# A graph-network kernel: in the edge-embedding pass TensorE makes the second product of the last group before the first product of the new one

## What is computed

```
def _mlp(h, W1, b1, W2, b2, g, beta):
    h = silu(h @ W1 + b1)
    h = silu(h @ W2 + b2)
    mu = mean(h, axis=-1); var = mean(square(h - mu), axis=-1)
    return g * (h - mu) * rsqrt(var + 1e-5) + beta

edge_attr = _mlp(edge_attr, emb_W1, emb_b1, emb_W2, emb_b2, emb_g, emb_beta)
...
agg = segment_sum(edges_new, dst)
```

## Time and profile before

| what | value |
|---|---|
| median of 3 runs | 4343.94 us (4342.17 to 4346.43) |
| the profiled execution's own time | 4335.36 us |
| span of its trace | 4333.6 us |
| share of the span: PE, DVE, ACT, POOL | 73%, 59%, 31%, 49% |
| the embedding pass, from PE's first product to ACT's last instruction | 195.7 to 679.6 us |

### The profile page before, as it was taken

The page is one execution under the profiler, slowest core; times in us unless marked ns, Lnnn a source line. Parts: engine busy times, 40 slices in busy tenths (PEclk is TensorE's granted clock), DMA queues, the critical chain, the costliest instruction groups (busy, mean ns, idle before and its releaser), DMA issues. The chain is left out here.

```text
span 4333.6 us, 75781 instructions
## 1 busy us (share of the span) xinstructions
PE 3180.2 (73%) x18633; PEld 2208.0 (51%) x18633; DVE 2559.6 (59%) x9494; ACT 1355.3 (31%) x2970; POOL 2130.8 (49%) x2173
## 2 busy tenths in 40 slices
PE   2488884669999997499998589998555555655554
PEld 1366662226666664377777367776333333333332
DVE  7678885986555563688887667776632222422223
ACT  0077875950111100255555345555300000200000
POOL 0477771000000001377775277776357777177776
PEclk7588987999999998599999799999755555755555
DMA  2112222000000002366666254455121212422223
GB/s 59 41 55 69 75 67 103 2 7 24 17 16 17 17 15 67 107 169 181 179 181 141 65 150 129 130 132 109 26 64 53 53 53 53 136 53 53 53 53 52
DMA packets 248988, 327.58 MB, mean 76 GB/s; under 512 B 78191, under 2 KB 159678, under 8 KB 247806
## 3 DMA queue, kind: packets, MB, share of 16 engines
q1 hardware_dynamic: 180410, 206.68, 15.5%
q0 software_dynamic: 68256, 117.02, 12.5%
HBM read 230.66 MB, written 92.83 MB: 75 GB/s over the span
## 5 line engine op out<-in xcount | busy, mean ns | idle before, releaser
L2520 PE MATMUL gat_acc<-gat_rows,gat_hot 128*128 128x128 f32 x1664 | 574.6, 478 | 486.0 <-issue 245.4
L2520 PEld LDWEIGHTS gat_acc<-gat_rows,gat_hot 128*128 128x128 f32 x1664 | 400.3, 317 | 661.6 <-issue 660.9
L992 PE MATMUL hop_p_a<-hop_h,adj 128*128 128x384 bf16 x4375 | 712.9, 327 | 0.0
L992 PEld LDWEIGHTS hop_p_a<-hop_h,adj 128*128 (+1 forms) x4375 | 428.5, 98 | 284.1 <-issue 1.7
L1928 POOL DMA_INDIRECT lb_far<-far_rows,lb_idx x416 | 405.6, 975 | 195.8 <-issue 117.0
L2503 POOL DMA_INDIRECT gat_rows<-typed_rows,gat_idx x416 | 395.7, 951 | 214.0 <-DVE gat_idx L2528 87.6
L2503 POOL DMA_INDIRECT gat_rows<-hidden_rows,gat_idx x416 | 395.2, 950 | 196.8 <-PE gat_acc L2520 77.4
L1928 POOL DMA_INDIRECT la_far<-far_rows,la_idx x416 | 409.7, 985 | 154.4 <-issue 117.9
L1650 POOL DMA_INDIRECT by_src_records<-scatter_rec,scatter_rank x375 | 376.9, 1005 | 128.9 <-issue 102.4
L2536 DVE TENSOR_SCALAR gat_hot<-iota_row,gat_tabs 128x128 f32<-128x128 f32 x416 | 147.7, 364 | 370.5 <-PE gat_acc L2520 364.4
L2533 DVE TENSOR_SCALAR gat_hot<-iota_row,gat_tabs 128x128 f32<-128x128 f32 x416 | 124.6, 305 | 392.6 <-PE gat_acc L2520 382.5
(11 more groups left out here) (498 smaller groups left out, 6418.9 us busy)
## 6 DMA issues: line engine op xcount, KB each, us to landing
edge_features<-emb_out SPq DMA_DIRECT2D x104, 256.0 KB
la_feat<-edge_features SPq DMA_DIRECT2D x104, 256.0 KB
edge_features<-la_out SPq DMA_DIRECT2D x104, 256.0 KB
lb_feat<-edge_features SPq DMA_DIRECT2D x104, 256.0 KB
la_place<-dst_row SPq DMA_DIRECT2D x104, 128.0 KB
lb_place<-dst_row SPq DMA_DIRECT2D x104, 128.0 KB
typed_rows<-gat_typed_row SPq DMA_DIRECT2D x25, 512.0 KB
hop_side<-x0share_nodes SPq DMA_DIRECT2D x125, 64.0 KB, 1.8
```

The source lines that it names most:

```text
L992: ins = nc.tensor.matmul(p_a[(u.par + r) % 2][:, 0:3 * D], K.adj[:, s, bass.ds(u.t * P, P)], h3[r % 2][:, s, :, :].rearrange("p i d -> p ( ...
L2520: nc.tensor.matmul(acc[:, bass.ds(at[u % LOADS], D)], hot[u % HOTS][:, :], rows[u % RING][:, :], start=False, stop=True, skip_group_check= ...
```

## The change

In each turn of PE's loop, `second(g-1)` is issued before `first(g)`; it was the other way round. The waits inside the two functions go with them. Nothing else is altered.

```
             for g in range(max(GE + SUM_LAG, ALL + 1)):
+                if 1 <= g <= ALL:
+                    second(g - 1)
                 if g < ALL:
                     first(g)
-                if 1 <= g <= ALL:
-                    second(g - 1)
                 if 0 <= g - SUM_LAG < GE:
                     third(g - SUM_LAG)
```

## The result

The changed kernel takes **4360.75 us** (median of 7 runs, 4359.49 to 4361.83). The kernel before, run again beside it, takes 4342.17 us (7 runs, 4335.14 to 4352.06). The ratio is 1.0041, with a 95% interval of 1.003 to 1.0052: 18.6 us slower, where 17.0 were forecast. The profiled execution took 4361.62 us, its span is 4359.8 us (4333.6 before).

A forecast was written before the change was run, and what follows sets the result against it. No engine is full in the middle of the pass; DVE was taken as pace maker. Losses of 5.9 + 10.1 + 1 = 17.0 us, added to the median 4343.94, gave 4360.9, taken as 4361 us, range 4348 to 4376.

The forecast's parts named there:

- The mechanism: On ACT, rows(g-1) is queued behind hidden(g), whose input now comes last; at both ends no third fills PE's gap.
- the three terms: Losses at start, middle and end of the pass: 5.9 + 10.1 + 1 = 17.0 us.
- Start: First six turns: PE waits for hidden(g) with no third between, 3.95 us a turn instead of 2.97; 5.9 us lost.
- Middle: Between the ends: rows comes 0.63 us later, lost only where DVE already waits for s, 16 times; 10.1 us.
- End: Last six turns, no third: 3.0 us more, partly taken back by emptier DMA queues; 1 us, between 0 and 3.
- The base: Whole kernel: the median of the runs shown, 4343.94 us, to which the forecast loss was added.
- (1): Middle: DVE's stock absorbs the late rows, loss shows only at the two ends; 4350.9 us, chance 0.13.
- (2): Middle: new DVE waits arise and PE's clock falls in more turns; up to 28 us, 4378, two thirds 4369; chance 0.19.
- (3): Middle: PE's pauses before L1684 close, its clock stays at 2.4 GHz, the kernel gets faster; 4332 us, chance 0.07.
- (4): On ACT: the exchange does nothing, as ACT is always behind and both inputs are there; chance counted into rival 1.

The follow-up runs named there:

- start_old_2: The changed kernel with the old order in the first seven turns of PE's loop, repeated on another chip; 5283.5 us, 1.0019 of the kernel before.
- rows_first: The changed kernel with ACT doing rows(g-1) ahead of hidden(g) in all turns; 5250.4 us, 1.0015 of the kernel before.
- apart_old: The kernel before, with PE's loop held back until POOL's scatter is through; 5277.59 us, 1.0073 of the kernel before.

## Why the prediction was right

**The mechanism** held in each place that was named: the order on ACT in the middle, and a chain of PE and ACT without `third` to fill it at both ends. How the middle's sum is made up was wrong in good part, and luck had a share in the total; both are below. ACT's waits moved from L1739 to L1722, `rows` follows `hidden` by 0.59 us (0.57 forecast), the first turns take 3.92 us (3.95), DVE's waits for `s` grew, and the phases behind the pass kept their lengths within 4 us. ACT's last instruction starts at 703.53 us where about 698 was forecast: 1.6 us of that lie before the pass, the rest in the three terms. The two by two table shows that the order on ACT is the cause in the middle, as the prediction argued from the earlier trace rows alone. It does not show it for the ends. There PE has lost its lead of one group, and exchanging ACT's order too made the end longer.

**Start**, forecast 5.9 us, measured 6.8. Each of six turns is 0.95 us longer, 5.7 in all, close to the forecast. The remaining 1.1 us were left out: `rows(0)` too now waits for `first(1)` and `hidden(1)`. The count should have been seven, the first at about this price.

**Middle**, forecast 16 x 0.63 = 10.1 us, measured 12.2. The sum is near, the make-up is not as it was put. The prediction let each of the 16 waits grow by 0.63 us, from 0.93 to 1.56, and took zero for all other groups. Matched group by group, only 10 of the 16 are still there, and grew by 0.27 us on average (2.7 us in all); 6 are gone (6.2 us); and 17 groups wait that did not (16.2 us). From group 58 on (478 us of the span) the waits come at every fourth group and take 0.82 to 0.91 us. So "where DVE does not wait, it has stock, and I take zero" is the step that failed, and the waits that were there gave less than nothing. The two errors went against each other, which is luck. What makes DVE run out of stock at every fourth group was not followed up. The 0.63 itself was rounded down on the way: 406.34 + 2.01 + 0.64 + 0.57 is 409.56, 0.70 us after 408.86, and 16 x 0.70 would have been 11.2 us.

**End**, forecast 1 us between 0 and 3, measured 1.7. The turns give 3.7 us instead of 3.0, since the products of L884 take 0.96 us up to the next start (699.04 to 700.00) where 0.86 were put in, and the full DMA queues take back 2.0 of it, as was argued. As said above, the two parts show in each trace; their sum, 1.7 and 1.2 us, is about what the old order's own ends differ by (38.4 to 39.7 us).

**The base.** The three terms came to 17.0 where the pass shows 20.7 and the medians 18.6. They were added to 4343.94, a median of three that lay 1.8 us above that of seven. So the forecast total, 4361, agrees with 4360.75 partly because a sum too small by 1.6 met a base too high by 1.8.

**The rivals.** (1), absorbed, falls with DVE's wait. (2), more lost than the waits of before, is there in its mechanism and not in its price: 17 groups in which DVE just had work now wait, DVE's wait about doubled (14.8 to 27.5 us by group, 30.5 in the window), which was its sign, and PE now waits 39 times for ACT's `out` ahead of its transposes (28.3 us) where it did 6 times (14.5 us), most of them in turns at full clock, where ACT starts the turn late because its first input comes last. But its second sign is missing: the clock is 0.86, not clearly below 0.87. Its price, two thirds of 28 us, was not paid. (3), faster by a clock kept up, showed half of its sign: PE's wait before L1684 fell from 54.9 to 36.5 us. Most of that reappears as the wait ahead of the transposes, 69.4 us for both before and 64.8 after, and the clock did not rise. Taken by itself that sign would have misled; it needed the sum of PE's waits. (4) falls with ACT's waits.

## What to carry to other kernels

An engine that takes its queue in order should find first the instruction for which the pace maker waits, once its input is ready; whoever exchanges two producers must look at the order of their consumers, and at each end of the loop apart, since there the work that fills the gap is missing. A mismatch that delays only the other consumer cost nothing in the middle here (392.5 us) and about 8 us at the end, with a part of that from a lower clock. The waits of the pace maker price such a change, but count also the groups in which it is only just not waiting: here 17 of the 27 were of that kind. When a wait on an engine shrinks, look whether it has moved to the instruction before.

## What the runs showed of the hardware that was not expected

*One pass, two paces.* On other chips the turns that run beside POOL's scatter take 25 to 29 us (six of them) and then about 61.6 us (five), in nearly all kernels alike. This was traced on two chips; on the third the kernel before takes as long, and in the traced kernels PE was held back. Busy time in `start_old_2`, most of this stretch, columns as above:

```profile
220.00:640.00 420.00, 44.83 (x161) 33.02 (x161) 25.01 (x128) 23.45 (x47) 306.74 (x316) 0.51 0.03 4
```

POOL is busy 307 of 420 us, about as in the earlier trace rows, PE 45 us, and the DMA engines 0.03 of the time. A typical instruction of ACT in `rows_first`:

```profile
490.56 0.60 ACT L1739 ACTIVATE emb_s<-emb_p_m 128x512 f32<-128x512 f32 x1 [55.21 <-remote]
```

It waits 55 us for something that the trace does not assign to an engine of the core. Held back until the scatter is through, the pass takes 498.5 us (`apart_old`, 675.6 to 1174.1 us), against 939 to 976 in the kernels that start it at 195 us, while the kernel becomes only 37 us longer: beside the scatter little more than the twelve slow turns get done. The pass explains some 450 of the 900 us by which the kernel before is slower on these chips. The rest lies behind it: 4092 to 4137 us from the store of the sums to the end, against 3647. The cause of both was not followed up and stays open.

*The clock.* PE busy 43 us more of 365 with products of three rows had the lower clock, 0.84 against 0.88. In this case busy time alone does not tell how long this engine is granted its upper level.
